# Causal attention on one core: products on 64 rows of TensorE issued in strict alternation between its two halves, and each causal mask's two pieces put on separate 64 by 64 quarters

## What is computed

```python
q, k = apply_p_rope(q, positions, D), apply_p_rope(k, positions, D)
attn = jnp.einsum('bhqd,bhkd->bhqk', q, k) / jnp.sqrt(D)
attn = jnp.where(jnp.tril(jnp.ones((T, T))).astype(bool), attn, finfo.min)
attn = softmax(attn, axis=-1)
y = jnp.einsum('bhqk,bhkd->bhqd', attn, v)
```

## Time and profile before

| what | value |
|---|---|
| median of the runs | 1144.67 us |
| span of the profiled execution, first to last instruction | 1139.4 us |
| TensorE matmul busy | 952.8 us, 84% |
| VectorE busy | 820.3 us, 72% |
| ScalarE busy | 701.6 us, 62% |
| GpSimd busy | 456.0 us, 40% |

### The profile page before, as it was taken

How to read it: one execution, slowest core, us unless ns; L and a number is a source line. 1 busy time by engine, 2 the same in 40 slices (tenths; PEclk the granted TensorE clock), 3 DMA queues, 4 the chain that set the end, 5 groups by cost and what they waited for, 6 DMA issues and landing times. The chain is left out here.

```text
span 1139.4 us, 26868 instructions
## 1 busy us (share of the span) xinstructions
PE 952.8 (84%) x9021; PEld 620.4 (54%) x9021; DVE 820.3 (72%) x2061; ACT 701.6 (62%) x1465; POOL 456.0 (40%) x526
## 2 busy tenths in 40 slices
PE   4675699999999999998678899984867769999993
PEld 2342243334333333344455688874655558999991
DVE  5888889999999999965866555556585874644434
ACT  3695277787888777775464566664602656666660
POOL 5807221223321122221277756561200176775441
PEclk9886599999999999999688999997968766999996
DMA  7235202111111100000321332639056233342216
GB/s 211 75 121 183 94 32 74 39 39 40 55 52 46 40 30 30 2 2 1 89 71 52 98 83 73 192 92 298 2 150 169 63 101 95 82 107 72 66 52 228
DMA packets 102430, 96.90 MB, mean 85 GB/s; under 512 B 15181, under 2 KB 85672, under 8 KB 102296
## 3 DMA queue, kind: packets, MB, share of 16 engines
q1 hardware_dynamic: 88120, 75.16, 22.9%
q0 software_dynamic: 8640, 17.84, 4.6%
q10 hardware_dynamic: 5536, 2.18, 0.7%
HBM read 60.05 MB, written 34.82 MB: 83 GB/s over the span
## 5 line engine op out<-in xcount | busy, mean ns | idle before, releaser
L569 DVE TENSOR_REDUCE part<-sps 128x2 f32<-128x1024 f32 (+2 forms) x307 | 327.5, 1114 | 25.6 <-PE sps L557 14.0
L912 ACT ACTIVATE prob<-tpa 128x1024 f32<-128x1024 f32 (+1 forms) x208 | 192.8, 927 | 45.4 <-PE tpa L858 43.6
L744 POOL TENSOR_SCALAR_AFFINE_SELECT prob<-prob 128x512 f32<-128x512 f32 x128 | 80.5, 641 | 306.2 <-ACT prob L912 306.2
L1791 POOL DMA_INDIRECT yk<-yo,place x142 | 144.7, 1019 | 104.1 <-ACT yo L1820 85.5
L1247 POOL DMA_INDIRECT xg<-pair,slot x128 | 127.2, 994 | 91.5 <-DVE slot L1398 53.5
L878 PE MATMUL ops<-prob,vs 128*32 128x512 f32 (+3 forms) x1536 | 157.9, 498 | 0.1
L912 ACT ACTIVATE prob<-tpb 128x512 f32<-128x512 f32 (+1 forms) x224 | 126.8, 566 | 35.2 <-PE tpb L858 35.1
L550 PE MATMUL sps<-qk 48*128 48x512 bf16 (+2 forms) x734 | 133.0, 339 | 12.3 <-DVE part L569 8.3
L1910 PE MATMUL banks<-xT,y 128*128 128x128 f32 x852 | 109.1, 279 | 1.6 <-ACT y L1805 0.7
L1848 DVE COPY place<-xt 128x1 uint32<-128x1 uint32 x142 | 21.7, 153 | 115.7 <-ACT esg L1814 77.9
L1910 PEld LDWEIGHTS banks<-xT,y 128*128 128x128 f32 x852 | 102.8, 195 | 2.8 <-issue 2.0
(11 more groups left out here) (365 smaller groups left out, 1870.9 us busy)
## 6 DMA issues: line engine op xcount, KB each, us to landing
xt<-xg SPq DMA_DIRECT2D x142, 65.0 KB
qk<-term SPq DMA_DIRECT2D x24, 256.0 KB, 2.7
qk<-qk SPq DMA_DIRECT2D x64, 96.0 KB
arena<-kpad SPq DMA_DIRECT2D x6, 1024.0 KB, 12.0
powers<-powr SPq DMA_DIRECT2D x8, 516.0 KB, 5.7
pair<-powers SPq DMA_DIRECT2D x8, 516.0 KB
qk<-qk SPq DMA_DIRECT2D x64, 64.0 KB
pair<-yk SPq DMA_DIRECT2D x8, 512.0 KB, 6.9
```

The lines of the kernel that those rows point to most:

```text
L569: return nc.vector.tensor_reduce(to, src, AX.X, ALU.max, negate=True)
L744: nc.gpsimd.affine_select(out=blk, in_=blk, pattern=[[0, HQ], [1, P]], compare_op=ALU.is_ge, fill=0.0, base=0, channel_multiplier=-1).then ...
L912: nc.scalar.activation(prob[:, at:at + len(units), 0:n], slot_of(t, m)[:, :, 0:n], ACT.Exp, scale=float(HD) ** -0.5).then_inc(exp_done, 1)
L1791: nc.gpsimd.indirect_dma_start(out=d.yk, out_offset=bass.IndirectOffsetOnAxis(ap=place[:, u:u + 1], axis=0), in_=yo[u][:], in_offset=None) ...
```

## The change

A small object, `Sides`, remembers the half used last and hands out pieces so that the halves alternate for as long as both have pieces left; it lives through all items of a phase. `row_scores` and `scores` take their matmuls from it. In `row_scores` one piece is either a score matmul or a mask, and a mask is two matmuls. These now load 64 identity columns instead of 128 and write 64 output rows instead of 128: piece u on the columns from 64u on, so on quarter (row 0 or 64, column 64u) of the array. The results are the same, since the columns left out only added zeros. Waits, semaphores, DMAs and the other engines are as before.

```diff
+class Sides:
+    def __init__(self):
+        self.last = 1
+    def __call__(self, *counts):
+        left, at = list(counts), [0, 0]
+        while any(left):
+            s = 1 - self.last if left[1 - self.last] else self.last
+            yield s, at[s]
+            left[s], at[s], self.last = left[s] - 1, at[s] + 1, s
...
-def row_scores(nc, w, t, n, out):
+def row_scores(nc, w, t, n, out, sides):
...
-    for at, x in enumerate(heads):
-        for s in range(2):
-            lo = 64 * s
-            ins = nc.tensor.matmul(out[:, s, at * wd:(at + 1) * wd], qk[lo:lo + KR, 0, x, i * P:(i + 1) * P],
+    per = len(heads) * (1 + diag)
+    for s, piece in sides(per, per):
+        at, mask = divmod(piece, 1 + diag)
+        x, lo, end = heads[at], 64 * s, (at + 1) * wd
+        if not mask:
+            ins = nc.tensor.matmul(out[:, s, at * wd:end], qk[lo:lo + KR, 0, x, i * P:(i + 1) * P],
                                    qk[lo:lo + KR, 1, x, c0:c0 + wd], start=True, stop=not diag,
                                    skip_group_check=True, tile_position=(lo, 0))
-        for u in range(2 * diag):
-            for s in range(2):
-                lo = 64 * s
-                ins = nc.tensor.matmul(out[:, s, (at + 1) * wd - P + 64 * u:(at + 1) * wd], w.half[lo:lo + 64, 0, u, :],
-                                       w.half[lo:lo + 64, 1, u, 64 * u:], start=False, stop=u == 1,
-                                       skip_group_check=True, tile_position=(lo, 0))
+        for u in range(2 * mask):
+            ins = nc.tensor.matmul(out[64 * u:64 * u + 64, s, end - P + 64 * u:end], w.half[lo:lo + 64, 0, u, 64 * u:64 * u + 64],
+                                   w.half[lo:lo + 64, 1, u, 64 * u:], start=False, stop=True,
+                                   skip_group_check=True, tile_position=(lo, 64 * u))
...
-                    for bank, (c, u) in enumerate(TITEMS[m]):
-                        s, x = UNITS[u]
-                        lo = 64 * s
-                        for j, q0, n, col in CHUNKS[c][1]:
-                            ins = nc.tensor.matmul(slot_of(t, m)[:, bank, col:col + n], ...
+                    parts = [[(bank, x, part) for bank, (c, u) in enumerate(TITEMS[m]) for sd, x in UNITS[u:u + 1] if sd == side
+                              for part in CHUNKS[c][1]] for side in range(2)]
+                    for s, piece in sides(len(parts[0]), len(parts[1])):
+                        (bank, x, (j, q0, n, col)), lo = parts[s][piece], 64 * s
+                        ins = nc.tensor.matmul(slot_of(t, m)[:, bank, col:col + n], ...
```

More of the change, by code:

```diff
@@ L453, in mod_rows @@
                     nc.tensor.matmul(out, csS[:, l, :], wm[:, l, cols], start=True, stop=True).then_inc(rows_ps, 1)
+                sides = Sides()
                 def maxima(first, last):
@@ L462, in maxima @@
                         after(pe, f_free, n - 1)
-                        row_scores(nc, w, 0, n, slot[n % 2]).then_inc(f_ready, 1)
+                        row_scores(nc, w, 0, n, slot[n % 2], sides).then_inc(f_ready, 1)
                 pe.wait_ge(id_in, 16)
@@ L787, in _ @@
             def _(pe):
-                used = [0]
+                used, sides = [0], Sides()
                 def acquire():
@@ L802, in s_item @@
                     out = acquire()
-                    filled(row_scores(nc, w, t, n, out))
+                    filled(row_scores(nc, w, t, n, out, sides))
                 def max_item(t):
@@ L853, in scores @@
                     after(pe, exp_done, prev + 1)
-                    for bank, (c, u) in enumerate(TITEMS[m]):
-                        s, x = UNITS[u]
-                        lo = 64 * s
-                        for j, q0, n, col in CHUNKS[c][1]:
-                            ins = nc.tensor.matmul(slot_of(t, m)[:, bank, col:col + n], qk[t % 4][lo:lo + KR + 2, 1, x, j * P:(j + 1) * P],
-                                                   qk[t % 4][lo:lo + KR + 2, 0, x, q0:q0 + n], start=True, stop=True,
-                                                   skip_group_check=True, tile_position=(lo, 0))
+                    parts = [[(bank, x, part) for bank, (c, u) in enumerate(TITEMS[m]) for sd, x in UNITS[u:u + 1] if sd == side
+                              for part in CHUNKS[c][1]] for side in range(2)]
+                    for s, piece in sides(len(parts[0]), len(parts[1])):
+                        (bank, x, (j, q0, n, col)), lo = parts[s][piece], 64 * s
+                        ins = nc.tensor.matmul(slot_of(t, m)[:, bank, col:col + n], qk[t % 4][lo:lo + KR + 2, 1, x, j * P:(j + 1) * P],
+                                               qk[t % 4][lo:lo + KR + 2, 0, x, q0:q0 + n], start=True, stop=True,
+                                               skip_group_check=True, tile_position=(lo, 0))
                     ins.then_inc(t_ready, 1)
```

## The result

Four runs of the changed kernel took 1170.09 to 1174.82 us, median 1174.16, where before has a median of 1144.81. The ratio is 1.0247 (95% interval 1.0228 to 1.0266), so it is 29 us slower.

A forecast was written before the change was run, and what follows sets the result against it. PE and DVE both nearly full in attention, neither the sole bound. 15 quads x 1.55 = 23 us plus half of 6 gave +26: span 1165.4, plus 5.3, 1171 us. Range: from +5 us to rival 1 with a dearer group.

The forecast's parts named there:

- Entry: Change of array shape from scores into a mask group: 0.095 us for each of 16 groups a quad.
- Exit and group: After masks: 0.095 us shape change for 12 of 16 groups; the group itself 0.10 us instead of 0.085.
- rival 3: Halves held in order, so alternation wins back 18 us over attention: net +8 us, 1153; chance 0.05.
- Alternation: New issue order of the halves in attention: costed at nothing, since each half already runs on by itself.
- The path: Attention quads: of 2.9 us added PE time, about 1.35 is absorbed and 1.55 us a quad stays.
- the walk: Pass through one quad, stretch by stretch, setting added shape changes against PE's pauses; leaves 1.55 us a quad.
- slack of 2.1: PE's true slack a quad: 0.72 us idle plus 1.4 us from record tails at some 9 waits.
- Rival 1: Shape changes in attention cost as forecast but next to nothing is absorbed: 49.5 us, 1194; chance 0.18.
- the first quad's score items: At 104 to 131 us, half clock: changes cost double, 6 us, of which half is left.
- rival 5: Clock falls to 1.2 GHz in attention as PE streams less densely: over 200 us; chance 0.02.
- around the span: Time outside the profiled span: 5.3 us, added to the forecast span of 1165.4 us.

The follow-up runs named there:

- e1: The changed kernel's alternation alone, with masks in their old shape of 64 rows by 128 columns: 1144.08 us, 0.9996 of the kernel before.
- e2: The kernel before with its order of issue, only the masks put on quarters: 1165.53 us, 1.0185 of the kernel before.
- e8: Old masks, opposite of alternation: within an item all matmuls of side 0 are issued, then all of side 1; 1146.00 us, 1.0012 of the kernel before.
- e6: The changed kernel with the masks of an item's two heads together at its end: 1156.79 us, 1.0099 of the kernel before.
- e7: The changed kernel with quarter masks in quads 0 and 1 only, old shape after, alternation everywhere: 1145.56 us, 1.0016 of the kernel before.
- e12: The kernel before with only the transpose of the maxima moved behind one transposed item, directly before a value item: 1144.24 us, 0.9994 of before.
- e5: The changed kernel with scores and transposed scores on quarters too, each product split into two matmuls of 64 output rows: 1146.61 us, 1.0029 of before.
- e13: The kernel before with the transpose of the maxima moved before a value item and both output transposes moved later, behind value items: 1157.24 us, 1.0107.

## Why the prediction was right

**Entry.** "One change, 0.095 us, for all 16 groups": it measures 0.10 in the rows above. The shapes 64 x 128 and 64 x 64 drain like the pairs in the earlier trace rows. The inference from a change of columns alone was sound. The sentence of the Trainium skill (TensorEngine Tiling (Array Packing), Key Properties) that a change of mode drains the engine holds here too.

**Exit and group.** The exit was forecast at 0.095 and the group at 0.10; they measure 0.12 and 0.06. Both were off by what the choice of where the masks' streaming ends moves between them. Together with the entry a group followed by scores adds 0.195 us (0.28 less 0.085; forecast 0.205), one followed by values 0.10 (from 319.47, the end of the scores, to 319.74 is 0.27, less the 0.175 of before; forecast 0.11). That makes 12 x 0.195 + 4 x 0.10 = 2.7 us a quad, where 2.9 was forecast. The 24 changes that rival 3 counts in a quad of before are 26 in the timeline (13 items of another shape, and the expectations' 25 and 53 are 26 and 54); the 28 added ones are right.

**Alternation.** Costed at nothing, and e1 shows nothing. The change is some 7 us slower than quarters without it (e2), which no term of the prediction covers and whose cause is open. Rival 3 fails on e8, where a half starts three matmuls ahead of its turn. So does the rule beside it, strict order of matmuls (the Trainium skill, TensorE: Matmul & The Clock Gate, Part 3).

**The path.** 1.55 of 2.9 us a quad was forecast to stay, by a walk through the pauses; 1.55 of 2.7 did on the mean, and 1.66 in the very quad of the walk (25.97 against 24.31). So some 1.1 us was absorbed, where 1.35 was forecast out of a slack of 2.1; that slack was built on 9 waits, of which the earlier trace rows list 13. The two long pauses of the earlier trace rows stand in the timeline of the change as follows:

```profile
329.58 0.39 PE L568 MATMUL sps<-qk 48*128 48x512 bf16 x2 [0.22 <-DVE part L585]
```

```profile
335.74 0.39 PE L874 MATMUL tpb<-qk 50*128 50x512 bf16 x1
336.03 0.39 PE L874 MATMUL tpa<-qk 50*128 50x512 bf16 x2
```

The second is 335.74 plus 0.21 of streaming to 336.03, so 0.08 us where it was 0.49, as the walk has it. The first shows 0.22 us idle where it showed 0.31, and shrank less than the walk has it. Counted from the transpose of the maxima (303.79 and 322.79), the scores behind it start at 6.79 instead of 6.39 us, 0.40 late where the walk has 0.11. Behind the second pause PE is 0.79 late (walk: 0.51), and the last stretch then adds less than the walk has. So the walk's total is right in part because two of its steps err in opposite directions; that part is luck. The form, pauses that take some changes while others cost nearly in full, is what e6 shows. Rival 1, full price throughout, is wrong by half.

**What failed.** The step "the first quad's score items ... I assume that a change costs double", +3 us up to the first transpose, was too high: PE's first transpose of maxima starts at 133.18 instead of 131.46, +1.7. In its place the clock came: rival 5 feared that it falls in attention, and it doesn't, but its rise came late, which no term of the sum had. Of the first quad's 8.2 us some 1 us is its changes of shape (the same quad lasts 26.4 us in e7, 0.8 over before), and the rest goes with the clock. The end of 1174 against a forecast of 1171 is therefore a right sum for the steady quads (23 us forecast for 15, 21.7 measured over 14) and luck in the rest. The sum lacks 6.6 us in the first quad (8.2 less the 1.55 it has) and 2.3 behind the last; against that stand terms that were too high, 1.3 us up to the first transpose and 3.8 us around the span (1.5 instead of 5.3).

## What to carry to other kernels

Count the changes of array shape in TensorE's order, not only the columns: each costs some 0.1 us here, also when only the number of columns changes, so smaller tiles cost something unless their neighbours have the same shape, and less if they are gathered behind one drain. Look at the starts, since two groups recorded with the same shape can still have the gap between them (e12). Before giving matmuls on separate row halves a finer order, look in the timeline whether one half already overtakes the other. Where two engines are nearly full, a sum over one of them doesn't price the loop: a pause behind an added piece can take all of it, without one it costs almost in full, and the one drain that e12 took away bought nothing.

## What the runs showed that was not expected

- The same masks on quarters cost 0.28 us between neighbours of 128 columns and 0.03 to 0.06 us between neighbours on quarters (e5). Splitting all 64-row products into twice as many matmuls cost about 0.3% (at most 0.5%), although PE issued 361 matmuls a quad instead of 265.
- In three profiles the step from 1.2 to 2.4 GHz came 12 to 18 us late, and in the change the quad around it lost 6.6 us more than a steady one, about as much as four steady quads of drains. The same matmuls up to that point had it on time in e7, so what delays it is open.
- Two output transposes moved by one or two items cost 13 us (e13), nearly half of what the change did.
